# One graph-network layer on one core: the first half of W_self loaded and split by row halves, a turned tile taken directly behind its centring, and the first products ordered by row half

## The reference

```python
h = jnp.maximum(_layernorm(x, axis=-1), 0.0)
xs = h[src]
for r in range(4):
    w_r = jnp.where(edge_type == r, edge_weight, 0.0)
    total_msg = total_msg + (xs @ W_rel[r] + b_rel[r]) * w_r[:, None]
agg = segment_sum(total_msg, dst, n)
deg = segment_sum(edge_weight, dst, n)
agg = agg / jnp.maximum(deg, 1.0)[:, None]
y = h @ W_self + b_self + agg
x1 = _layer_norm(h + y, ln1_g, ln1_b)
ffn = gelu(x1 @ W_ffn1 + b_ffn1) @ W_ffn2 + b_ffn2
out = x + _layer_norm(x1 + ffn, ln2_g, ln2_b)
```

## Time and profile before

| | us |
|---|---|
| median of 3 runs | 245.69 (245.59 to 247.01) |
| the profiled execution, its own time | 243.86 |
| its span, first to last instruction | 242.1 |
| around the span (243.86 less 242.1) | 1.76 |
| PE busy in the span | 232.5 (96%) |
| mean granted TensorE clock | 0.996 |

### The profile page before, as it was taken

The page is one execution under the profiler, slowest core; times in us unless marked ns, Lnnn a source line. Parts: engine busy times, 40 slices in busy tenths (PEclk is TensorE's granted clock), DMA queues, the critical chain, the costliest instruction groups (busy, mean ns, idle before and its releaser), DMA issues.

```text
span 242.1 us, 4104 instructions
## 1 busy us (share of the span) xinstructions
PE 232.5 (96%) x1695; PEld 193.2 (80%) x1695; DVE 181.2 (75%) x338; ACT 65.6 (27%) x86; POOL 16.6 (7%) x36
## 2 busy tenths in 40 slices
PE   7699999999999999999999999999999999999990
PEld 7588778777787778887887878788899999887890
DVE  3769859799996877796799698739529789655564
ACT  3742425245153043102102202313315533100000
POOL 8020000000000000000020020002000000011111
PEclk9999999999999999999999999999999999999998
DMA  6888620305004200000000000003700870002111
GB/s 184 231 211 140 210 83 3 89 12 169 0 2 176 91 0 3 0 8 1 3 5 3 0 8 0 3 5 106 240 4 0 230 202 0 1 20 67 43 42 42
DMA packets 10376, 15.95 MB, mean 66 GB/s; under 512 B 2930, under 2 KB 3680, under 8 KB 10354
## 3 DMA queue, kind: packets, MB, share of 16 engines
q1 hardware_dynamic: 10172, 15.49, 22.7%
q10 hardware_dynamic: 182, 0.16, 0.2%
HBM read 14.22 MB, written 1.28 MB: 64 GB/s over the span
## 4 chain that ended last, share of the span: by engine, by line
PE 91%; issue 3%; DMA 3%; DVE 1%; SPq 1%; ACT 0%; POOL 0%; POOLq 0%; DVEq 0%
PE ps L1007 89%; DMA stage<-in_L_gnn_W_self 3%; PE ps L1095 1%; PE ps L1014 1%; SPq L354 1%; ACT wring L488 0%; POOL small L471 0%; DVE small L991 0%; DVE t2buf L990 0%; POOLq L177 0%; DVE ybuf L983 0%; DVEq L177 0%; DVE small L972 0%; DVE small L974 0%
## 5 line engine op out<-in xcount | busy, mean ns | idle before, releaser
L1007 PE MATMUL ps<-wring,hT 128*125 128x512 f32 x300 | 72.8, 398 | 1.6 <-ACT wring L488 1.5
L1007 PEld LDWEIGHTS ps<-wring,hT 128*125 128x125 f32 x300 | 54.6, 185 | 14.7 <-ACT wring L488 1.7
L1007 PE MATMUL ps<-T_hi,AT_hi 125*125 125x512 f32 x100 | 40.3, 403 | 0.0
L1007 PE MATMUL ps<-T_lo,AT_hi 125*125 125x512 f32 x100 | 39.4, 394 | 0.0
L706 DVE TENSOR_TENSOR eqp<-iota_p,pairs 128x1638 f16<-128x1638 f16 x25 | 25.1, 1005 | 2.6 <-issue 1.3
L1007 PE MATMUL ps<-T_hi,AT_lo 125*125 125x512 f32 x100 | 26.0, 403 | 0.0
L516 ACT CAST AT_hi<-ps 128x1500 fp32r<-128x1500 f32 (+1 forms) x10 | 12.3, 1234 | 48.7 <-PE ps L1007 48.6
L1007 PEld LDWEIGHTS ps<-kw,eqp 128*128 128x128 f16 x650 | 19.4, 97 | 6.5 <-issue 6.3
L1007 PE MATMUL ps<-kw,eqp 128*128 128x40 f16 (+1 forms) x650 | 21.8, 190 | 0.3 <-issue 0.2
L1007 PEld LDWEIGHTS ps<-T_lo,AT_hi 125*125 125x125 f32 x100 | 18.6, 186 | 4.2
L1007 PEld LDWEIGHTS ps<-T_hi,AT_hi 125*125 125x125 f32 x100 | 18.5, 185 | 4.2
(11 more groups left out here) (125 smaller groups left out, 278.5 us busy)
## 6 DMA issues: line engine op xcount, KB each, us to landing
stage<-in_L_gnn_W_rel SPq DMA_DIRECT2D x8, 512.0 KB, 3.7
stage<-in_L_gnn_W_ffn SPq DMA_DIRECT2D x8, 512.0 KB, 4.3
x<-in_x SPq DMA_DIRECT2D x5, 224.0 KB
x_again<-in_x SPq DMA_DIRECT2D x5, 224.0 KB
stage<-in_L_gnn_W_self SPq DMA_DIRECT2D x2, 512.0 KB, 7.1
out<-ybuf SPq DMA_DIRECT2D x4, 224.0 KB
g_bc<-in_L_gnn_ln_g SPq DMA_DIRECT2D x2, 256.0 KB, 6.5
b_bc<-in_L_gnn_ln_b SPq DMA_DIRECT2D x2, 256.0 KB, 7.2
```

The source lines that it names most:

```text
L1007: return nc.tensor.matmul(o, l, r, start=start, stop=stop, skip_group_check=True)
```

## The change

- **Loads.** Unit 0 is loaded by two DMAs of 256 KB in place of one of 512 KB, at the same place of SP's order: row block k = 0 signals a new semaphore `first_in`, row block k = 1 signals `stage_in` of buffer 0.
- **High parts.** ACT copies the two row blocks apart (`first_high(0)`, `first_high(1)`, 128x512 each); the first signals `first_hi`, the second `w_hi`. They stand between `hT_high(0)`, `hT_high(1)` and `h_of(2)`.
- **ACT's order.** `hT_high(2)` comes directly behind `h_of(2)`, `hT_high(3)` directly behind `h_of(3)`, and so on, where before `h_of(3)` stood ahead of `hT_high(2)` and `h_of(4)` ahead of `hT_high(3)`.
- **Low parts.** DVE subtracts the two row blocks apart: the first behind `hT_low(0)`, the second behind `row_mean(3)`. `hT_low(1)` now comes ahead of `row_mean(3)`.
- **First products.** `first_product(k, s)` is two matmuls with row block k of unit 0: high and low of the tile. For tiles 0 and 1 it takes the place of `product_hi`: k = 0 first, then k = 1. The wait for `w_hi` stands ahead of k = 1 alone.
- **Dummies.** The two dummies behind `turn_h(2)` are gone.

```diff
-    WARM = [10, 3, 2]
+    WARM = [10, 3]
...
-            load(0)
+            sp.dma_start(stage_view(0)[:, 0, :], units[0][0][:, 0, :]).then_inc(first_in, 16)
+            sp.dma_start(stage_view(0)[:, 1, :], units[0][0][:, 1, :]).then_inc(stage_in[0], 16)
...
+            def first_high(k):
+
+                if k == 0:
+                    act.wait_ge(first_in, 16)
+                    a.copy(units[0][1][:, 0, :], stage_view(0)[:, 0, :]).then_inc(first_hi, 1)
+                else:
+                    act.wait_ge(stage_in[0], 16)
+                    a.copy(units[0][1][:, 1, :], stage_view(0)[:, 1, :]).then_inc(w_hi, 1)
...
             hT_high(0)
-            high_part(0)
+            first_high(0)
             hT_high(1)
+            first_high(1)
             h_of(2)
+            hT_high(2)
             h_of(3)
-            hT_high(2)
+            hT_high(3)
             h_of(4)
-            hT_high(3)
             hT_high(4)
...
             hT_low(0)
+            dve.wait_ge(first_hi, 1)
+            v.tensor_tensor(units[0][2][:, 0, :], stage_view(0)[:, 0, :], f32(units[0][1][:, 0, :]),
+                            ALU.subtract).then_inc(first_lo, 1)
+            hT_low(1)
             row_mean(3)
-            hT_low(1)
-            low_part(0)
+            dve.wait_ge(w_hi, 1)
+            v.tensor_tensor(units[0][2][:, 1, :], stage_view(0)[:, 1, :], f32(units[0][1][:, 1, :]),
+                            ALU.subtract).then_inc(w_lo, 1)
             hT_low(2)
...
                 if s == 0:
                     pe.wait_ge(w_lo, u + 1)
+                if s == 0 and u == 0:
+                    pe.wait_ge(first_lo, 1)
...
+            def first_product(k, s):
+
+                if s == 0 and k == 0:
+                    pe.wait_ge(first_hi, 1)
+                if s == 0 and k == 1:
+                    pe.wait_ge(w_hi, 1)
+                if k == 0:
+                    pe.wait_ge(hT_a, s + 1)
+                mm(ps[0:TN, s, :], hT_all[:, 0, 0, k, s, :], wring[:, 0, 0, k, :], k == 0)
+                if k == 0:
+                    pe.wait_ge(hT_b, s + 1)
+                mm(ps[0:TN, s, :], hT_all[:, 0, 1, k, s, :], wring[:, 0, 0, k, :], False)
...
             dummies(WARM[1])
-            product_hi(0, 0)
+            first_product(0, 0)
+            first_product(1, 0)
             turn_h(2)
-            dummies(WARM[2])
-            product_hi(0, 1)
+            first_product(0, 1)
+            first_product(1, 1)
             product_lo(0, 0)
```

More of the change, by code:

```diff
@@ L214, in gnn_layer @@
         h_act = sem("h_act")
+        first_in = sem("first_in")
+        first_hi = sem("first_hi")
+        first_lo = sem("first_lo")
         w_hi = sem("w_hi")
```

## The result

The changed kernel takes **242.75 us** (median of 6 runs, 242.38 to 242.97), the kernel before beside it 245.64 (6 runs, 243.65 to 247.01). The ratio is 0.9897, with a 95% interval of 0.9859 to 0.9935: 1.0% faster, 2.5 us. The ratio is an estimate of its own; the two medians lie 2.89 us apart.

The account below looks back on a forecast made before the run. PE's own work was taken as the bound. Centring of tile 2 earlier (0.88) and dummies gone (0.37) made 1.25, less 0.05 is 1.2 us off the median 245.69: 244.5 us, range 243.6 to 246.0.

Parts of the forecast that it names:

- What bounds the kernel: From 15.29 to 229.50 us PE's own work bounds; an earlier change is worth what it moves that dense part earlier.
- The landing of the first half: Load of unit 0: first half lands at 7.45 us, between bounds of 7.17 and 8.42, second near 8.42.
- ACT's steps: Early ACT work: half copies take 0.61 us and block 0.52; centring of tile 2 starts at 8.98, 0.88 earlier.
- The dummies' 0.37: On PE behind the transposes of tile 2: removing the two dummies gains 0.37 us.
- Is what follows ready: Tiles 3 and 4: ACT and DVE feed PE in time; low part of second half at 10.97, cover 0.25 us.
- SP's longer queue costs nothing: SP's loads: one DMA more, 0.48 us of issue, is covered by at least 1.7 us at the load ACT awaits.
- Rival 1: Load of unit 0: both halves land together at 8.42; gain 0.3 us, time 245.4; chance 0.10.
- Rival 2: Later in the run: gain lost against something unmoving, such as the load at 25.50; 245.7 or 246.2 us; chance 0.07.
- Rival 3: Tile 3 of x lands late, delaying DVE's second low part and PE; 0.45 us slower, 246.1; chance 0.04.
- the sum: Whole run: 1.2 us less than the median 245.69 gives 244.5; less than the profiled 243.86 gives 242.7.
- The fast bound: Whole run: PE's idle 1.46 and the dummies' 0.37 make 1.83 us, so not under 243.8 but by scatter.
- Rival 4: PE near 9 us: clock falls to 1.2 of 2.4 GHz; 1.9 us more, 0.7 slower net, 246.4; chance 0.03.

Follow-up runs that it names:

- the repeated run: The changed kernel timed again with no edit, beside the kernel before: 242.66 us (12 executions, 242.16 to 243.84).
- three added profiles: The kernel before, unchanged, profiled three more times: 245.49, 246.29 and 245.60 us.

## Why the prediction was wrong, point by point

- **What bounds the kernel.** Right. PE's dense body begins earlier and nothing behind takes any of it back: 1.54 at tile 4, 1.54 at the picks, 1.50 at the last long piece. The other profiles agree: in 17 of the 18 the time of the execution is 228.3 to 228.8 us more than the start of the transposes of tile 4, whatever came ahead of them (in the one with ACT's old order it is 229.2).
- **The landing of the first half**, taken as 7.45: it was 7.16 in the profiled execution, and the first copies of the other kernels with the split load began between 7.10 and 7.89. Right as a middle, but the landings scatter; the forecast gave a range for where it lands and none for how it moves between executions.
- **ACT's steps.** Right in size: the half copies took 0.62 (forecast 0.61), start to start 0.53 and 0.52 (0.52). They began 0.3 us earlier than forecast, and so did the centring of tile 2, at 8.69 against 8.98. That is the 1.17 of tile 2 against my 0.88, and most of what separates 1.54 from 1.2 in the profiles.
- **The dummies' 0.37.** Right: tile 2 to tile 3 took 1.95 where it took 2.32. Put back they cost 0.37 in a profile and 0.52 in the medians.
- **Is what follows ready.** Right in the main. The low part of the second half stood at 10.79 (forecast 10.97), the centring of tile 3 began at 10.63 (10.91), tile 4 came 2.33 behind tile 3. But the cover of 0.25 for the low part wasn't there: PE's weight load waited 0.23 us for it (0.29 in the repeated run), and the six matmuls took 1.55 where 1.47 were counted. The transposes took 0.40 in place of 0.48, which hid this in the sum.
- **SP's longer queue costs nothing.** Right, and the load I was wary of came earlier and not later: ACT's copy of it began at 24.19, before 25.50. Rivals 1, 2 and 3 didn't happen.
- **The step that failed** is the sum, where the 1.2 us of one profiled execution were taken off a median that lies "1.83 above the profiled one", as if the changed kernel would lie as far above its own. It lies 0.37 above (242.75 less 242.38). The 1.83 come from the clock, and in the three low executions that were profiled from a late landing too. The profile of before shows an execution in which both were good; in 59 of 121 the mean clock is low, and those take 1.9 us more. The change takes all of them away (0 of 12 in the one group, and a clock of 0.991 and over in each of the first six). As an estimate, half of 1.9 is 0.9, and with 1.7 at the high clock that is 2.6, against 2.5 by the ratio and 2.9 by the medians. The fast bound had the same fault: "not under 243.8" takes the whole of the hole and the dummies off that same median.
- **Rival 4** had the mechanism, on the wrong kernel. Its price of 1.9 us was put as "3.8 us of work" at the low level; at half the clock that much work would take 3.8 more, and 1.9 is the loss in a stretch that lasts 3.8. The stretch itself cost 1.35 to 1.47 in the three profiles. That the two sets of executions also lie 1.9 apart is luck, as late landings are in that figure. "Against it: the clock held through the longer one" rested on a single execution. The Trainium skill, "TensorE: Matmul & The Clock Gate", section "Part 4: PE-mode transpose", says that a transpose doesn't count as PE-busy in the same way, which would make the dummies beside the transposes worth having. The runs of the kernel before fit that (10 of 12 low without them, 11 of 33 beside it with them), but they don't show that it is the reason: dummies at another place did as well (1 of 12), and in the changed kernel none of 12 is low with or without them.

What isn't settled: what makes the clock fall in one execution and not in another with the same hole. A wait of 2.33 us went by at 1.00 in one profile, and two of 0.73 and 0.62 brought the low level in another. Nor is it settled how many of the low executions of before also had a late landing: the three that were profiled all had one.

## What to carry to other kernels

A profile is one execution. Where a median lies well above the profiled time, look at the mean granted clock of every run before taking a gain off the median: here it split the runs of one kernel into two sets 1.9 us apart. Then profile one execution of the slower set, as the distance of the sets can hold more than the clock (here 1.35 to 1.47 us of it, the rest a late landing). A hole in PE's work costs its own length and, in some executions, a stretch at half the clock behind it; dummies put into it test this cheaply, and here five of them, with no other edit, took 1.4 us off the median, about half of the 2.9 between the medians of before and changed in the same group.

## What the runs showed of the hardware that was not expected

- In two of the three added profiles of the kernel before the half clock came just ahead of the first matmul behind the wait, in the third one 0.8 us behind it, when PE was at work again; it lasted to between 13.3 and 14.3 us and ended under full work.
- The landing of the same 512 KB, issued at about 2.1 us each time, came between 8.42 and 9.5 us in the kernel before, and that of a first half between 7.10 or earlier (in one profile ACT began to copy it then without a wait) and some 7.9.
- One DMA more on SP's queue didn't push the later ones back: the issue of unit 3 began at 20.45 in the changed kernel, at 21.57 in the profile of before, and between 21.09 and 22.30 in its three added profiles.
